# Linear stage: turning every second tile's rounded rows by a DMA transpose instead of on TensorE

## The reference

```python
def _quant_e4m3(t):
    amax = jnp.max(jnp.abs(t)).astype(jnp.float32)
    scale = jnp.maximum(amax / E4M3_MAX, 1e-12)
    fp8 = (t.astype(jnp.float32) / scale).astype(jnp.float8_e4m3fn)
    return (fp8, scale)
...
x = x + _L0_xattn_ref(_layernorm(x, axis=-1), ctx_512, L0_xattn_Wq, L0_xattn_Wkv_expand, L0_xattn_Wout)
x = x + _L0_ffn_ref(_layernorm(x, axis=-1), L0_ffn_weight)
```

## Time and profile before

| | |
|---|---|
| median of 3 runs | 1797.81 us (1797.55 to 1800.09) |
| the profiled execution | 1799.89 us, span 1798.1 us |
| PE busy, of the span | 97% |
| DVE, ACT, POOL busy | 75%, 38%, 10% |
| linear stage, first transpose to the last record of the span | 1540.8 to 1798.1 us |
| one tile of the linear stage | 3.90 us |

### The profile page before, as it was taken

The page is one execution under the profiler, slowest core; times in us unless marked ns, Lnnn a source line. Parts: engine busy times, 40 slices in busy tenths (PEclk is TensorE's granted clock), DMA queues, the critical chain, the costliest instruction groups (busy, mean ns, idle before and its releaser), DMA issues.

```text
span 1798.1 us, 26754 instructions
## 1 busy us (share of the span) xinstructions
PE 1744.1 (97%) x10698; PEld 842.0 (47%) x10730; DVE 1343.6 (75%) x1844; ACT 689.0 (38%) x643; POOL 185.3 (10%) x143
## 2 busy tenths in 40 slices
PE   8689999999999999999999999999999999799998
PEld 4434454445444544454445444544454443455554
DVE  6776778677866787778777877787778665777776
ACT  5632133223322332233223322332233221788886
POOL 0000000000000000000000000000000011355555
PEclk9899999999999999999999999999999999899999
DMA  9664545454545354545454545454544444777763
GB/s 317 158 185 118 136 105 129 117 137 104 129 117 140 100 129 117 124 117 129 117 124 117 129 117 125 116 129 117 124 117 117 117 112 122 267 270 268 269 245 140
DMA packets 371689, 263.96 MB, mean 147 GB/s; under 512 B 322320, under 2 KB 324880, under 8 KB 371088
## 3 DMA queue, kind: packets, MB, share of 16 engines
q1 hardware_dynamic: 371600, 262.71, 53.7%
HBM read 119.28 MB, written 71.30 MB: 106 GB/s over the span
## 4 chain that ended last, share of the span: by engine, by line
PE 91%; issue 5%; DVE 2%; ACT 1%; DMA 1%; POOL 0%; SPq 0%; POOLq 0%; DVEq 0%
PE ps_all L623 70%; PE ps_all L760 12%; PE ps_all L610 2%; PE ps_all L632 2%; PE ps_all L596 1%; PE ps_all L597 1%; PE ps_all L693 1%; PE ps_all L575 1%; DVE n_buf L1066 1%; ACT tile_space L844 0%; ACT n_buf L832 0%; DMA tile_space<-tile_space 0%; DVE amax L1045 0%; DMA tile_space<-in_ctx_dram 0%; PE ps_all L565 0%
## 5 line engine op out<-in xcount | busy, mean ns | idle before, releaser
L623 PE MATMUL ps_all<-m_buf,tile_space 128*128 128x512 f16 x3072 | 681.6, 381 | 4.7 <-DVE wo_t L1267 4.7
L623 PE MATMUL ps_all<-n_buf,tile_space 128*128 128x512 f16 x3024 | 670.0, 379 | 0.0
L623 PEld LDWEIGHTS ps_all<-m_buf,tile_space 128*128 128x128 f16 x3072 | 298.5, 98 | 368.9 <-issue 13.1
L623 PEld LDWEIGHTS ps_all<-n_buf,tile_space 128*128 128x128 f16 x3024 | 292.1, 98 | 350.1 <-issue 6.2
L760 PE MATMUL ps_all<-wo_t,tile_space 128*128 128x512 bf16 x992 | 231.1, 381 | 2.8 <-DVE tile_space L1377 1.2
L858 ACT ACTIVATE tile_space<-tile_space,neg_mean 128x1024 f32<-128x1024 f32 x63 | 72.4, 1149 | 327.6 <-DVE neg_mean L1153 327.6
L514 POOL TENSOR_TENSOR rstd_x<-veps_x,minus_half 128x1 f32<-128x1 f32 x64 | 35.3, 551 | 1388.2 <-DVE veps_x L1096 1388.2
L854 ACT ACTIVATE tile_space<-tile_space,score_scale 128x1024 f32<-128x1024 f32 x64 | 73.5, 1148 | 230.9 <-DVE tile_space L1123 230.9
L760 PEld LDWEIGHTS ps_all<-wo_t,tile_space 128*128 128x128 bf16 x1024 | 97.8, 98 | 107.7 <-issue 1.7
L850 ACT ACTIVATE tile_space<-tile_space 128x1024 f16<-128x1024 f32 x64 | 67.6, 1057 | 184.5 <-DVE tile_space L1133 184.5
L1083 DVE SCALAR_TENSOR_TENSOR tile_space<-tile_space 128x1024 f16<-128x1024 f32 x64 | 78.4, 1225 | 64.0 <-ACT tile_space L850 64.0
(11 more groups left out here) (128 smaller groups left out, 1700.6 us busy)
## 6 DMA issues: line engine op xcount, KB each, us to landing
tile_space<-in_x_dram SPq DMA_DIRECT2D x128, 512.0 KB, 3.8
x_scratch<-tile_space SPq DMA_DIRECT2D x64, 512.0 KB, 3.0
m_buf<-x_scratch SPq DMA_DIRECT2D x32, 512.0 KB, 4.0
tile_space<-x_scratch SPq DMA_DIRECT2D x32, 512.0 KB, 4.0
out_dram<-m_buf SPq DMA_DIRECT2D x32, 512.0 KB, 2.9
out_dram<-tile_space SPq DMA_DIRECT2D x31, 512.0 KB, 2.9
m_buf<-in_L_xattn_Wq_dram SPq DMA_DIRECT2D x4, 1024.0 KB, 11.1
n_buf<-in_L_xattn_Wout_dram SPq DMA_DIRECT2D x2, 2048.0 KB, 18.3
```

What stands on the lines that cost most here:

```text
L623: mm = nc.tensor.matmul(to[:, cols], left[:, ls, c * P:(c + 1) * P], right[:, rs, c, cols], start=(c == 0 and i == 0), stop=(c == CT - 1 a ...
```

## The change

Tile 0 and all even tiles are turned on PE as before; tile 1 too. The odd tiles from 3 to 63 are rounded into one of four buffers (`rows_buf`, in the space of `wq_stack`), turned by a DMA transpose that SP issues (`turn_rows`) into one of four buffers (`turned_buf`), and read from there by the matmuls. The tiles are quantised in the order 0, 1, 3, 2, 5, 4, 7, 6 and so on (`tile_of`); the product keeps the order 0, 1, 2, 3. n below is the number in the order of quantising: for an even n from 2 on it is tile n + 1, for an odd one tile n - 1. So the rounding of tile 2k is number 2k + 1.

```diff
+            def turn_rows(t):
+                k = t // 2
+                sp.wait_ge(r_ready, t)
+                if k >= 5:
+                    sp.wait_ge(y_full, 2 * k - 6)
+                sp.dma_start_transpose(turned_buf[:, k % 4].rearrange("p (c r) -> p c r", r=P),
+                                       rows_buf[:, k % 4]).then_inc(rows_turned[k % 4], 16)
+
+            turn_rows(3)
+            for t in range(T - 1):
+                if t % 2 == 0 and t + 5 < T:
+                    turn_rows(t + 5)
+                store_out(t, t % X2)
+                if X2 <= t + X2 - 1 < T:
+                    reload((t - 1) // X2, (t - 1) % X2)
...
+            def linear_pair(q, i, last=False):
+                t = q * 8 + 2 * i
+                k = q * 4 + i
+                pe.wait_ge(rt_ready, k + 2)
+                linear(t, 0, rt_t[(i + 1) % 2])
+                pe.wait_ge(rows_turned[i], q * 16 + 16 if i else q * 16)
+                linear(t + 1, 1, turned_buf[:, i],
+                       None if last else lambda: turn_r(t + 4, k + 2, i % 2))
...
-            def magnitudes(t, i, e, first=False):
-
+            def magnitudes(n, j):
+                e = j % 2
+                t, i = tile_of(n, e), tile_of(j, e) if isinstance(n, int) and n < 2 else j + 1 - 2 * e
...
-            def quantise(t, e, first=False):
-                shifted(t + 1, 1 - e)
-                copy_rt(t, e, first)
-                rounded(t + 1, 1 - e)
...
+            def quantise_pair(q, i):
+                k = q * 4 + i
+                shifted(2 * k + 2, 0)
+                copy_rt(k + 1, (i + 1) % 2, {1: 1, 2: 2}[k] if isinstance(k, int) and k < 3 else 2 * k - 3)
+                if not (isinstance(k, int) and k < 4):
+                    dve.wait_ge(rows_turned[(i + 1) % 4], q * 16)
+                rounded(2 * k + 2, 0, rows_buf[:, (i + 1) % 4])
+                shifted(2 * k + 3, 1)
+                dve.wait_ge(r_full, k + 1)
+                rounded(2 * k + 3, 1, r_t[i % 2])
```

More of the change, by code:

```diff
@@ L268, in xattn_ffn_kernel @@
         rt_ready = sem("rt_ready")
+        rows_turned = [sem(f"rows_turned{k}") for k in range(4)]
         y_full = sem("y_full")
@@ L285, in xattn_ffn_kernel, with tile_of @@
         y_t = [tile_space[:, 12, :].bitcast(BF16)[:, i * H:(i + 1) * H] for i in (0, 1)]
+        rows_buf, turned_buf = (wq_stack[:].rearrange("p h c -> p (h c)")[:, i:i + 4 * H].bitcast(BF16)
+                                .rearrange("p (k c) -> p k c", k=4) for i in (0, 4 * H))
+        def tile_of(n, parity):
+            return n if isinstance(n, int) and n < 2 else n + 1 if parity == 0 else n - 1
         y_ps = [ps_all[:, 0:H], ps_all[:, HALF:HALF + H]]
@@ L741, in _, with turn_r, linear @@
                 turn_w8(a)
-            def turn_r(t, e, first=False):
-                pe.wait_ge(r_ready, t + 1)
+            def turn_r(count, m, buf, first=False):
+                pe.wait_ge(r_ready, count)
                 if not first:
[L747 to L751, removed]
+                    pe.wait_ge(rt_ready, m)
+                turn(r_ps, r_t[buf], r_full, ident_bf)
+            def linear(t, e, left, between=None):
                 for k in range(2):
@@ L759, in linear @@
                     for c in range(CT):
-                        mm = nc.tensor.matmul(y_ps[e][:, cols], rt_t[e][:, c * P:(c + 1) * P], w8_t[:, c, cols],
+                        mm = nc.tensor.matmul(y_ps[e][:, cols], left[:, c * P:(c + 1) * P], w8_t[:, c, cols],
                                               start=(c == 0), stop=(c == CT - 1))
@@ L771, in _ @@
             pe.wait_ge(x1_ready, T + 1)
[L772 to L779, removed]
+            turn_r(1, 0, 0, True)
+            pe.wait_ge(rt_ready, 1)
+            linear(0, 0, rt_t[0], lambda: turn_r(2, 1, 1))
+            pe.wait_ge(rt_ready, 2)
+            linear(1, 1, rt_t[1], lambda: turn_r(4, 2, 0))
+            for i in range(1, 4):
+                linear_pair(0, i)
+            with pe.Fori(1, T // 8 - 1) as q:
+                for i in range(4):
+                    linear_pair(q, i)
+            for i in range(4):
+                linear_pair(T // 8 - 1, i, last=(i == 3))
         @block.scalar
@@ L975, in _ @@
             for t in range(AHEAD):
-                magnitudes(t, t, t % 2, t < 2)
+                magnitudes(t, t)
                 if t >= 2:
-                    values(t, t, t % 2)
+                    values(t, t)
             act.wait_ge(quant_ready, 3)
@@ L984, in step2 @@
                 scaled(t, i % 2, first)
-                magnitudes(t + AHEAD, ahead, ahead % 2)
-                values(t + AHEAD, ahead, ahead % 2)
+                magnitudes(t + AHEAD, ahead)
+                values(t + AHEAD, ahead)
             for t in range(2):
@@ L1363, in shifted, with rounded @@
                                                op1=ALU.add).then_inc(a_done, 1)
[L1365 to L1370, removed]
-                                               op1=ALU.subtract).then_inc(r_ready, 1)
[L1373 to L1377, removed]
+            def rounded(n, e, to):
+                dve.wait_ge(a_done, n + 1)
+                nc.vector.scalar_tensor_tensor(out=to, in0=u_ps[e], scalar=ROUND_LEAST, in1=a_t[e], op0=ALU.max,
+                                               op1=ALU.subtract).then_inc(r_ready, 1)
@@ L1379, in _, with copy_rt @@
+            def copy_rt(m, buf, tiles_done=None):
+                dve.wait_ge(r_full, m + 1)
+                if tiles_done is not None:
+                    dve.wait_ge(y_full, tiles_done)
+                nc.vector.tensor_copy(rt_t[buf], r_ps).then_inc(rt_ready, 1)
             first_values(0)
             shifted(0, 0, True)
-            rounded(0, 0, True)
+            rounded(0, 0, r_t[0])
             first_values(1)
-            copy_rt(0, 0, True)
+            copy_rt(0, 0)
             shifted(1, 1, True)
-            rounded(1, 1, True)
@@ L1387, in quantise @@
-            def quantise(t, e, first=False):
-                shifted(t + 1, 1 - e)
-                copy_rt(t, e, first)
-                rounded(t + 1, 1 - e)
[L1392 to L1397, removed]
+            rounded(1, 1, r_t[1])
+            shifted(2, 0)
+            copy_rt(1, 1)
+            rounded(2, 0, rows_buf[:, 1])
@@ new lines, in _ @@
+            shifted(3, 1)
+            dve.wait_ge(r_full, 1)
+            rounded(3, 1, r_t[0])
+            def quantise_pair(q, i):
[8 more added lines that the diff above has]
+                rounded(2 * k + 3, 1, r_t[i % 2])
@@ L1398, in _ @@
+            for i in range(1, 4):
+                quantise_pair(0, i)
+            with dve.Fori(1, T // 8 - 1) as q:
+                for i in range(4):
+                    quantise_pair(q, i)
+            for i in range(3):
+                quantise_pair(T // 8 - 1, i)
+            copy_rt(T // 2, 0, T - 5)
             dve.wait_ge(got_x1[X2 - 1], 16 * (T // X2))
```

11 lines of the change are left out of this document (6 added, 5 removed).

## The result

| | before | changed |
|---|---|---|
| median of 5 runs | 1798.28 us (1797.55 to 1800.09) | 1834.29 us (1834.04 to 1835.47) |
| profiled execution | 1799.89 us, span 1798.1 | 1834.29 us, span 1832.5 |

The ratio is 1.020, with a 95% interval of 1.0188 to 1.0212: the changed kernel is 36.0 us slower. 1832.7 had been predicted, +34.9 on a median of 1797.81.

A forecast was written before the change was run, and what follows sets the result against it. PE was taken to bound the kernel, ACT working in step with it. Start +1.09, thirty pairs +34.2 and end -0.45 gave +34.9 us on 1797.81, so 1832.7 us; range 1820 to 1842, chance 0.80.

The forecast's parts named there:

- The bound and its reach: Linear stage: PE busy 97% of the span; 8 transposes fewer save 0.45 us of 7.80 a pair if all else fits.
- The first loop: End of linear(2k) through ACT, DVE's shifted and copy to linear(2k + 2): 5.53 us against 3.90, 8.98 us a pair.
- The second loop: Through rounding 2k + 3 and PE's transposes: 8.42 us a pair; as a rival holding alone, 1817 us, chance 0.05.
- The start and the end: Linear stage: tile 2 turned 1.09 us late, first two pairs 8.4 us each, the end 0.45 us shorter.
- the sum: Whole kernel: start +1.09, thirty pairs +34.2, end -0.45, together +34.9 us.
- The turned rows: SP's DMA transposes stay off the path: 1.7 us issue, 4 to landing, 11.4 cover; late landing as rival, 0.04.
- the 16-block row: Earlier DMA transposes of 16 blocks, 3.42 us issue, 5.3 landing; bounds for 8 blocks: 1.7 to 3.4 and 3.5 to 7.1.
- The DMA share: DMA engines in the linear stage: 7.7 us needed a pair, 0.86 of 8.98, more than all of 7.35.
- a rival: Linear stage: the saving arrives, 7.35 us a pair, 1785 us, up to 1793 with DMA engines short; gain chance 0.07.
- The clock: PE's clock stays 1.00; rival: waits drop it to 1.2 GHz, 12.4 us a pair, 1937 us, chance 0.02.

The follow-up runs named there:

- e2_lead5: The changed kernel with ACT making magnitudes and values 5 numbers ahead of scaled instead of 4: 1787.14 us, ratio to before 0.9933.
- e8: The changed kernel plus one 128x1024 f32 DVE multiply per pair, between shifted number 2k + 2 and copy_rt: 1872.12 us.
- e10: The changed kernel plus one 128x512 DVE multiply per pair, between shifted number 2k + 2 and copy_rt: 1844.02 us.
- e9: The changed kernel plus one 128x1024 f32 DVE multiply per pair, at the end of the pair behind rounded number 2k + 3: 1833.76 us.
- e1_copy_first: The changed kernel with DVE's copy_rt ahead of shifted number 2k + 2 in each pair instead of behind it: 1818.42 us, ratio to before 1.0111.
- e6_lead5_transposes_twice: The changed kernel with ACT's lead 5 instead of 4 and every linear-stage DMA transpose issued twice, both waited for: 1808.76 us, ratio to before 1.0058.
- e7_all_by_dma: The kernel before with all tiles but tile 0 turned by DMA, natural rounding order, ACT's lead 5, reloads two tiles later: 1777.64 us, ratio 0.9885.
- e5_transposes_twice: The changed kernel with every linear-stage DMA transpose issued a second time to a spare buffer, both waited for: 1834.45 us.

## Why the prediction was right, point by point

*The bound and its reach.* Right. Taking transposes off PE is worth its 0.45 us a pair only where nothing else is near, and e2_lead5 shows that worth: 7.35 us a pair instead of 7.80.

*The first loop.* Right in place and size. 5.53 + 3.45 = 8.98 us a pair was predicted, 8.98 measured. The single hops in the fences above: matmuls to scaled 0.22 (1642.94 and 3.45 to 1646.61), 1.01, 1.13, v's 1.23, 0.04, shifted to copy 1.14, copy to matmul 0.73 to 0.81. e8 and e10 lengthen it by 0.60 and about 0.3 us and the pair follows; e9 puts the same work where DVE idles and nothing follows.

*The second loop.* Right. 8.42 was predicted for it alone; e1_copy_first, which leaves it alone, runs at 8.40 and gives 1818.4 us.

*The start and the end.* The transposes of tile 2 are at 1550.20 in a linear stage that began 0.92 us earlier (1539.86 against 1540.78), so they were 1.18 us late, where 1.09 was predicted. The 30 pairs to 1818.77 took 268.6, predicted 268.2; the first two took 8.47 and 8.61, where 8.4 each had been worked out. What follows them, from the transposes of tile 62, took 13.7 us, 14.2 before. Together the stage grew by 35.3 us, 34.9 in the sum; its start 0.92 us earlier leaves the 34.4 between the two profiled executions.

*The turned rows.* Right that they stay off the path; the transfers were cheaper than I took them: 1.23 us of issue and 3.1 to landing, where I took 1.7 and 4. The row of all 31:

```profile
L488 SPq DMA_TRANSPOSE wq_stack<-wq_stack x31: 1232/1233/1905, 1547.7 to 1814.7; - x31
...
DMA to landing us min/median/max: 3.0/3.1/4.7
```

So 8 blocks land in 3.1 us with other transfers in flight, which decides against the 1309 ns a block that I had quoted from the Trainium skill, VectorE: DVE Perf Modes, section The three transpose paths, at least for blocks in one transfer. My own bounds from the 16-block row were too high too: the issue was below 1.7 and the landing below 3.5, and for half the blocks the median issue was 0.36 of the other median. That row runs from 1451 to 5137 ns for the same 16 blocks, and 8 blocks took 1.23 us here and 4.09 at most in e6_lead5_transposes_twice: the issue has no fixed price by the number of blocks, so that half of a median was no floor.

*The DMA share.* 0.86 was predicted, 0.85 measured. But the step behind it, that 7.7 us of DMA time a pair could not fit into 7.35, was wrong: e2_lead5 ran at 7.35 with a share of 1.05, which is just these 7.7 us, and e7_all_by_dma at 7.0 (the 63 products from linear(1) on, begun at 1550.6, take 220.5 us) with 1.09. The sum was right, and 1 wasn't its limit. It touched only a rival.

*The clock.* Right for the change, and nearer to wrong than its 0.02 says. It stayed at 1.00 through the waits of 1.42 to 1.51 us that the trace shows, and fell in e8 after 2.0 to 2.2 us, in some pairs and not in others. The Trainium skill, TensorE: Matmul & The Clock Gate, section HAM oscillation, tells of a kernel with such a loss in every pass; the trace of the change shows none, and e8 shows one in 12 steps of 29.

*What stays open.* The medians are 36.0 us apart and the two profiled executions 34.4, with 34.9 predicted; the runs of one kernel differ by more than that (1797.55 to 1800.09). Why e8's clock falls after one wait of 2.0 us and not after the next isn't settled by these runs, and neither is why SP's issue of a transpose takes 1.2 us in one kernel and 2.2 in another.

## What to carry to other kernels

When work leaves the engine that bounds a loop, or its order is changed, follow each operand round the whole ring of queues, and count how many products lie between the event that releases it and the one that needs it: here that lead fell from two tiles to one, 5.5 us of latency no longer fitted, and the engines' busy shares showed nothing of it. The remedy was then a matter of one number (the lead) or of the order of two lines, and both cost nothing; but a longer lead is not free in itself, since an instruction that waits for a buffer holds up everything behind it on its engine. A wait on TensorE has a second price, its clock: 1.8 us cost 1.8, and 2.1 cost up to 3.8.

## What had not been expected of the hardware

- A DMA share of 1.05 to 1.09 didn't mean that the DMA engines were the limit. At 1.05 and 329 GB/s e2_lead5 lost nothing, nor did e5_transposes_twice at 1.07 and 292, and e7_all_by_dma moved 384 GB/s at 1.09; e6_lead5_transposes_twice at 1.07 to 1.10 and 302 to 313 GB/s did wait for its transposes. The share doesn't tell them apart; the order of SP's queue and PE's waits have to be looked at.
- A wait of 2.0 to 2.2 us in every pair pulled TensorE's clock to 1.2 GHz in 12 steps of 29, for about 3.4 us each (8 weight loads 0.43 us apart), and so did a single one of 2.22 us in e6_lead5_transposes_twice; waits of 1.75 to 1.85 us in every pair didn't.
